# Matmuls on constants ahead of eight kinds of waits on TensorE

## What is computed

```python
xn = _layernorm(x)                     # block 0
s = _L0_attn_ref(xn, ...)              # selective scan, 16 states, forward and backward
g = _silu(_L0_ffn_ref(xn, ...))        # router over 8 experts, top 2, and a 128-512-128 gelu FFN
x = x + s * g
xn = _layernorm(x)                     # block 1
s = _L1_attn_ref(xn, ...)              # Mamba-2 style layer: conv, chunked SSD, gated norm
g = _silu(_L1_ffn_ref(xn, ...))        # 2 layers: 8 heads, local windows of 64, then a gated gelu FFN
x = x + s * g
```

## Time and profile before

| | |
|---|---|
| median of three executions | 4375.0 us |
| the profiled execution: its own time | 4371.11 us |
| its span, from the first to the last instruction | 4369.2 us |
| TensorE busy | 3325.9 us (76%) |
| ScalarE busy | 2576.3 us (59%) |
| VectorE busy | 2492.6 us (57%) |
| GpSimd busy | 1724.1 us (39%) |
| TensorE's mean granted clock | 0.903 of full speed |

### The profile page before, as it was taken

How to read it: one execution, slowest core, us unless ns; L and a number is a source line. 1 busy time by engine, 2 the same in 40 slices (tenths; PEclk the granted TensorE clock), 3 DMA queues, 4 the chain that set the end, 5 groups by cost and what they waited for, 6 DMA issues and landing times. The chain is left out here.

```text
span 4369.2 us, 57389 instructions
## 1 busy us (share of the span) xinstructions
PE 3325.9 (76%) x17248; PEld 1950.3 (45%) x17248; DVE 2492.6 (57%) x4239; ACT 2576.3 (59%) x5843; POOL 1724.1 (39%) x1428
## 2 busy tenths in 40 slices
PE   4677778777777777777777787777777777777776
PEld 2344444444444444444444454444444444445443
DVE  6554655656555565656556555565565656566433
ACT  4455556565665655556655565656656556565554
POOL 2253442534334353343533435244243433435332
PEclk9798899998989889898998989989999898999999
DMA  2000000000000000000000000000000000000000
GB/s 79 3 1 1 5 1 6 1 1 6 1 6 1 1 6 1 6 1 1 6 1 6 1 6 1 1 6 1 6 1 1 6 1 6 1 1 3 1 3 3
DMA packets 18387, 20.57 MB, mean 5 GB/s; under 512 B 768, under 2 KB 17152, under 8 KB 17792
## 3 DMA queue, kind: packets, MB, share of 16 engines
q1 hardware_dynamic: 18048, 16.44, 1.1%
HBM read 12.24 MB, written 4.19 MB: 4 GB/s over the span
## 5 line engine op out<-in xcount | busy, mean ns | idle before, releaser
L1441 POOL TENSOR_TENSOR hc<-hst,Cs 128x512 f32<-128x512 f32 x512 | 654.6, 1278 | 1231.3 <-DVE hst L1211 1167.9
L1211 DVE TENSOR_TENSOR_SCAN hst<-dA,bank 128x512 f32<-128x512 f32 x512 | 624.9, 1220 | 314.3 <-ACT dA L901 150.5
L556 PE MATMUL bank<-W,xs 128*128 128x512 f32 x960 | 521.3, 675 | 140.9 <-DVE tmp L1352 137.7
L907 ACT COPY Cs<-bank 128x512 f32<-128x512 f32 x512 | 299.0, 584 | 313.2 <-PE bank L539 284.6
L1203 DVE TENSOR_TENSOR bank<-u,bank 128x512 f32<-128x512 f32 x512 | 351.4, 686 | 208.5 <-PE bank L539 207.2
L1500 POOL TENSOR_TENSOR oT<-tmp 128x512 f32<-128x512 f32 x256 | 324.5, 1268 | 347.7 <-DVE tmp L1352 198.1
L539 PE MATMUL bank<-parts,sel 96*128 96x512 bf16 x1024 | 370.9, 439 | 112.8 <-DVE hst L1211 42.2
L1515 POOL TENSOR_TENSOR Pm<-Pm,rinv 128x512 f32<-128x512 f32 x256 | 271.0, 1058 | 419.5 <-DVE rinv L1365 400.3
L1037 ACT ACTIVATE Pm<-bank,mx 128x128 f32<-128x128 f32 x1024 | 364.0, 373 | 112.9 <-DVE mx L1372 112.7
L901 ACT ACTIVATE dA<-delta,neg_a 128x512 f32<-128x512 f32 x512 | 371.3, 725 | 48.5 <-DVE hst L1211 47.6
L524 PE MATMUL bank<-C,hc 128*128 128x128 f32 x2048 | 365.7, 309 | 36.3 <-POOL hc L1441 36.3
(11 more groups left out here) (223 smaller groups left out, 6117.1 us busy)
## 6 DMA issues: line engine op xcount, KB each, us to landing
W<-wpack SPq DMA_DIRECT2D x1, 4498.0 KB, 13.2
x_tok<-x SPq DMA_DIRECT2D x16, 256.0 KB, 2.9
out<-xa SPq DMA_DIRECT2D x16, 256.0 KB, 2.2
rot<-tables SPq DMA_DIRECT2D x2, 512.0 KB, 15.9
wc_f<-taps SPq DMA_DIRECT2D x1, 1024.0 KB, 19.1
C<-cpack SPq DMA_DIRECT2D x1, 721.0 KB, 14.5
Pm<-mask SPq DMA_DIRECT2D x1, 320.0 KB, 14.8
tmp<-rowpack SPq DMA_DIRECT2D x1, 256.0 KB, 17.0
```

What stands on the lines that cost most here:

```text
L556: mm(b[:, :], weights, rhs, start=True, stop=True).then_inc(full(ring, job), 1)
L907: nc.scalar.copy(Cs[:, k % 2, :], b[:, :]).then_inc(sem("a_Cs"), 1)
L1211: v.tensor_tensor_scan(o, a, b, 0.0, ALU.mult, ALU.add).then_inc(sem("a_h"), 1)
L1441: g_.tensor_tensor(hc[:, k % 2, :], hst[:, k % 2, :], Cs[:, k % 2, :], ALU.mult)\
```

## The change

A helper issues n bf16 matmuls of 128x512 whose operands are the constants `ident16` and `mask16`. It is called at eight kinds of places, each time after TensorE has waited for the bank and before it waits for data. Where the two waits stood the other way round, their order is turned. The results are overwritten by the job that follows (`start=True`). Per item these are 10 (down) + 8 (mdt) + 6 (st) + 2 for each of 16 turns + 4 and 3 for each of two layers' norm sums + 8 for each of two layers' first `fg`: 86 matmuls, 1376 over 16 items.

```diff
+            def keep_busy(b, n):
+                for _ in range(n):
+                    mm(b[:, :], ident16[:, :], mask16[:, 0:T], start=True, stop=True)
...
                 def down(m):
-                    pe.wait_ge(*step("a_h1", i, m + 1))
                     if m == 0:
                         if later(i):
                             pe.wait_ge(*before("a_y", i))
+                        keep_busy(y_acc, 10)
+                    pe.wait_ge(*step("a_h1", i, m + 1))
...
-            def norm_sum(ring, job, i, weights, rhs):
+            def norm_sum(ring, job, i, weights, rhs, first=None, fill=0):
                 if used(ring, job, i):
                     pe.wait_ge(*vacant(ring, job, i))
                 b = bank(ring, job)
+                if first:
+                    keep_busy(b, fill)
+                    pe.wait_ge(*first)
                 mm(b[:, :], weights, rhs, start=True, stop=True).then_inc(full(ring, job), 1)
...
-                pe.wait_ge(*step("m_h", i))
                 if used("A", "mdt", i):
                     pe.wait_ge(*vacant("A", "mdt", i))
                 b = bank("A", "mdt")
+                keep_busy(b, 8)
+                pe.wait_ge(*step("m_h", i))
...
-                pe.wait_ge(*step("m_bt", i))
-                pe.wait_ge(*step("m_xdd", i))
                 for q in range(3):
                     if used("B", f"st{q}", i):
                         pe.wait_ge(*vacant("B", f"st{q}", i))
                     b = bank("B", f"st{q}")
+                    if q == 0:
+                        keep_busy(b, 6)
+                        pe.wait_ge(*step("m_bt", i))
+                        pe.wait_ge(*step("m_xdd", i))
...
                     def turn(n):
-                        pe.wait_ge(*step("t_P", i, NU * l + n + 1))
                         if used("B", f"PT{l}_{n}", i):
                             pe.wait_ge(*vacant("B", f"PT{l}_{n}", i))
                         b = bank("B", f"PT{l}_{n}")
+                        keep_busy(b, 2)
+                        pe.wait_ge(*step("t_P", i, NU * l + n + 1))
...
-                    pe.wait_ge(*step("f_xs", i, 2 * l + 2))
-                    norm_sum("B", f"lmean{l}", i, centre[:, :], xs0[:, 0:T])
+                    norm_sum("B", f"lmean{l}", i, centre[:, :], xs0[:, 0:T], step("f_xs", i, 2 * l + 2), 4)
                     yield at_l + UNITS_END + 2
-                    pe.wait_ge(*step("f_sq", i, l + 1))
-                    norm_sum("B", f"lvar{l}", i, inv128[:, :], tmp2[:, 0, :])
+                    norm_sum("B", f"lvar{l}", i, inv128[:, :], tmp2[:, 0, :], step("f_sq", i, l + 1), 3)
                     yield at_l + UNITS_END + 3
-                    pe.wait_ge(*step("f_hn", i, l + 1))
...
                             b = bank("B", f"{kind}{l}{m}")
+                            if kind == "fg" and m == 0:
+                                keep_busy(b, 8)
+                                pe.wait_ge(*step("f_hn", i, l + 1))
```

## The result

The changed kernel takes 4391.7 us in the median of eight runs, against 4375.4 us: the ratio is 1.0041, with a 95% interval of 1.0031 to 1.0050. It is slower by 16 us. One of the eight runs before, at 4959 us, was in a slow state, far above the rest, and is not in the ratio; without it their median is 4375.0 us. The forecast was 4379 us with no difference that can be told; the time lies in the range and in the forecast's own range, 13 us above the number. The profiled execution took 4391.26 us, its span is 4389.3 us, 20.1 us longer than before.

A forecast was written before the change was run, and what follows sets the result against it. No single engine bounds the kernel: TensorE is busiest at 76% but waits on the others in turn, losing clock. Terms summed to +0.05 us per round and +4.3 us outside, giving 4379 us; range 4305 to 4430 us, the forecast's own 4355 to 4405.

The forecast's parts named there:

- the clock at the fills: Signs of being right: mdt's matmuls near 290 ns, mean clock 0.93 to 0.95, TensorE busy some 290 us longer.
- the 1.8 of the term: Behind mdt: 8 hidden fills keep the clock up, so ScalarE starts 1.8 us earlier; range 0 to 3.1 us.
- Down: Ahead of down: 10 fills hidden in the wait, a later clock fall gives back 0.7 us per round.
- Turns: 2 fills at each of 16 turns: partly on the path, +1.1 us per round, between 0 and 6.9.
- Layer 1's end: Norm sums and first fg of layer 1: fills on the path cost 0.4 + 1.3 us per round.
- st: 6 fills ahead of st: delay against earlier return of the clock, net -0.7 us, between +1.5 and -2.2.
- Layer 0's end: Norm sums and first fg of layer 0: fg's fills hidden, the end costs 0.65 us per round.
- The last item: Where no scan stands beside the units: turns cost +7.7 us, warmer fg phases give -3.4, together +4.3 us.
- Sum per round: All terms of a round added: +1.1 + 2.35 - 0.7 - 1.8 - 0.7 - 0.2 = +0.05 us, nothing.
- (b): Rival: fills stand in the path, clock gains end in waits; 4431 or 4414 us, rounds over 269 us; chance 0.22.
- Rival (c): Rounds lock: one that ends earlier may find the next wait longer; 4375 us whatever the fills do; chance 0.07.
- The price of a fill: Spacing of 512-column bf16 matmuls: about 0.22 us at full clock, 0.43 at half; 86 fills are 18.6 us per item.

The follow-up runs named there:

- e1: Changed kernel with only the fills at down (10), mdt (8) and st (6), none at turns and layer ends: 4366.2 us, 0.9982 of the kernel before.
- e0: Changed kernel with every fill count set to 0, only the turned order of the two waits left: 4394.5 us, 1.0047 of the kernel before.
- e5: e1 with 4 more fills ahead of the first convolution matmul, as plain delay of 0.86 us per round: 4417.5 us, 1.0090 of the kernel before.
- e6: e1 with 12 more fills ahead of the first convolution matmul, as plain delay of 2.6 us per round: 4416.9 us, 1.0095 of the kernel before.
- e2: Changed kernel with only the 2 fills ahead of each turn: 4420.1 us, 1.0102 of the kernel before.
- e3: Changed kernel with only the fills at the layer ends (lmean 4, lvar 3, fg 8): 4429.4 us, 1.0128 of the kernel before.
- e7: e1 with 24 fills into the idle accumulator ahead of the 5.66 us wait for the bank of xt1: 4334.0 us, 0.9907 of the kernel before.
- e11: The whole change plus 24 fills ahead of the wait for the bank of xt1: 4349.1 us, 0.9946 of the kernel before.
- e12: The whole change without the 8 fills ahead of fg in layer 1: 4371.0 us, 0.9993 of the kernel before.

## Why the prediction was right or wrong, step by step

**What it said of the clock at the fills was right.** The stretches behind down and mdt are gone, mdt's matmuls have 256 ns (I had said near 290), the mean clock is 0.927 (said: 0.93 to 0.95) and TensorE is busy 197 us more (said: 290; I forgot what the faster clock takes off). ScalarE's wait behind mdt is what was forecast, 2.84 for 4.60 us:

```profile
2501.22 0.60 ACT L1012 ACTIVATE Pm<-bank 128x512 f32<-128x512 f32 x1 [2.84 <-PE bank L564]
```

From mdt's first matmul to that square are 2.06 us instead of 3.82, the 1.8 of the term. But these 1.8 us do not reach the end of the round. The projection matmuls that start at 249.57 us before start at 247.36 in the short round, 2.2 us ahead, and the next round begins at 266.22 instead of 266.23. From 245 us on the round now has 10.2 us at half clock (6.83 from 245.98, 3.41 from 259.63), where before it had 3.4 (from 249.77): in place of the fall at mdt there are falls later, in work that others wait for. The first scores of layer 1 take 1.92 us instead of 1.05, and VectorE waits 2.41 us for them instead of 1.10. TensorE's lines, after and before:

```profile
2530.55 1.92 PE L736 MATMUL bank<-kT,qbd 128*128 128x128 f32 x8
```

```profile
2251.99 1.05 PE L725 MATMUL bank<-kT,qbd 128*128 128x128 f32 x8
```

**Terms that held.** Down: from its first matmul to layer 1's fg are 23.12 us in e1 and 23.57 before, 0.45 of the 0.7 taken. Turns: down comes 0.85 us later than in e1 (30.87 against 30.02; taken 1.1), but at layer 1's output projection only 0.16 us are left of it. Layer 1's end: from lmean to L1411 (before: L1399) 16.8 us instead of 15.5, so 1.3 where the terms had 1.7. The residual of the layer in the short round, beside it:

```profile
2333.52 1.53 DVE L1411 SCALAR_TENSOR_TENSOR yB<-bank,W,xs 64x512 f32<-64x512 f32 x2 [0.21 <-PE bank L813]
```

**Terms that were off.** st: from xt1 to the y norm's matmul (L675, now L686) e1 needs 13.55 us and before 13.36; -0.7 was taken and +0.2 came. Layer 0's end: +0.65 was taken; from lmean to fg it is 6.97 instead of 7.18 us. The last item: +4.3 was taken; from the last round's start to the end it is 512.0 instead of 514.8 us, -2.7. The order of the waits has no term at all; its price was put at nothing without a reason, and without fills it is 20 us (e0).

**The step that failed** is the one that looked safest: "Sum per round". The terms are real where they arise, but they do not add up to the round. A lead of up to 2 us in a round vanishes before its end (e1 and the changed kernel, whose next round begins where it did), and 0.86 us more in the wrong place becomes 3.2 (e5). So the sum of +0.05 us was near to what six of the 13 rounds show, none, and blind for the seven that grew by 3.4. Rounds longer than 269 us were one of the prediction's own signs of being wrong, in favour of (b); they came, but (b) would have lengthened every round, and three times the delay gave no longer rounds (e6).

That the total came within 13 us is partly luck. The same terms taken in parts missed by 39 us (e1: 4327 said, 4366 measured), 23 (e2: 4397, 4420) and 22 (e3: 4407, 4429).

Rival (c) was this mechanism and had 0.07 of the chance; it too was half told, since I let it only absorb ("whatever the fills do") and not tip. The runs that settle that terms do not add up are e5 and e6. Why time is absorbed they do not settle. One place where a gain goes is read above, behind mdt. For lost time the traces show this much: in e1's rounds the start of stage B varies by 0.6 us (78.77 and 79.38 in two neighbours) and the convolution behind it by 0.37 (85.21 and 85.58). Between the two lies the end of a half-clock stretch, at 82.0 us in the one and 82.1 in the other, so it does not move with the start, and a late start leaves fewer matmuls at half clock. I take this as the cause, but it was read, not tested. Nor is it tested why lengths 3.4 us apart are preferred; the stretches at half clock are 3.42 us or a multiple of it long, which points to the clock.

The price of a fill was right at full clock: six in 1.46 us and 24 in 5.34 us are 0.216 us each plus a fixed end. In the traces of the changed kernel, e1 and e7 no two matmuls of 512 columns start less than 215 ns apart, so the 131 ns per matmul that the Trainium skill gives for a stream ("TensorE: Matmul & The Clock Gate", "Back-to-back issue gap") are not seen; the measured spacing decides. The rule of the Trainium skill on pauses between bursts of matmuls (same page, "Loop structure matters more than you think") agrees with e7: with the longest pause of a round filled (5.66 us), the half-clock stretch behind it is gone. A better clock alone is not less time: e11 has the better clock and the worse time.

## What to carry to other kernels

Where TensorE's clock falls in waits of a repeating pattern, do not add up microseconds of edits: see whether rounds have a few preferred lengths, and test with a known small delay how close the pattern stands to its next length. Fill the wait that begins a long half-clock stretch with work behind it, and leave alone waits shorter than the fill and banks that come free last (e12, e3, e2). A higher granted clock or a busier TensorE is no evidence of a shorter time.

## What was not expected of the hardware

Rounds of nearly the same work came most often near 262.8 (e7), 266.2 (before, e1), 269.6 (e2) and 269 or 273 us (e3), so about 3.4 us apart. The order of pairs of waits, with nothing else changed, moved the median by 20 us and spread the runs over 20 us, where those of before and e1 spread over 12 and 13. Two rounds of one execution that lay 0.06 us apart at one matmul ended 3.4 us apart. A gain behind one filled wait (1.8 us at mdt) was lost again in the same round, to a half-clock stretch that came later.
